# Masked cross attention: pairs of heads on halves of 64 rows, mask addition and maximum in one instruction, the output in a projection bank

## The reference

```python
h = _rmsnorm(hidden_states, ln1_w)
kv = _rmsnorm(kv_states, ln1_w)
q = (h @ Wq).reshape(bsz, q_len, NH, HD).transpose(0, 2, 1, 3)      # 16 heads of 64
k = (kv @ Wk).reshape(bsz, k_len, NKV, HD).transpose(0, 2, 1, 3)    # 4 heads of 64
v = (kv @ Wv).reshape(bsz, k_len, NKV, HD).transpose(0, 2, 1, 3)
q = _apply_rope(q, cos_q, sin_q)
k = _apply_rope(k, cos_k, sin_k)
k, v = repeat of each of the 4 heads for 4 query heads
scores = jnp.einsum('bhqd,bhkd->bhqk', q, k) / math.sqrt(HD)
scores = scores + attention_mask                                    # (8, 1, 112, 375)
probs = jax.nn.softmax(scores.astype(jnp.float32), axis=-1)
attn = jnp.einsum('bhqk,bhkd->bhqd', probs, v)
hidden = residual + attn.transpose(0, 2, 1, 3).reshape(bsz, q_len, NH * HD) @ Wo
```

## Time and profile before

| | us |
|---|---|
| three runs: median (lowest to highest) | 2206.13 (2204.8 to 2211.46) |
| the profiled execution | 2202.19 |
| its span | 2200.4 |
| TensorE matmul busy in the span | 1836.1 (83%) |
| VectorE | 1396.9 (63%) |
| ScalarE | 877.2 (40%) |
| GpSimd | 640.2 (29%) |
| mean granted clock of TensorE | 0.915 |

### The profile page before, as it was taken

One profiled execution on the slowest core, in us unless ns is written; L12 is line 12 of the kernel. 1 busy time (PEld: TensorE's weight loads), 2 busy tenths in 40 slices (PEclk: granted clock), 3 DMA queues, 4 the chain that ended last, 5 costly groups with the idle time before them and its releaser, 6 DMA issues.

```text
span 2200.4 us, 34499 instructions
## 1 busy us (share of the span) xinstructions
PE 1836.1 (83%) x10658; PEld 1321.1 (60%) x10658; DVE 1396.9 (63%) x3343; ACT 877.2 (40%) x2513; POOL 640.2 (29%) x710
## 2 busy tenths in 40 slices
PE   5969997399848779998879998877887779988978
PEld 4747775388736567776745554663445655655557
DVE  5856666111168756666756676676777876777765
ACT  4635553122236425554334443333332354444421
POOL 2235553200033335555300000220002243544433
PEclk9979998599969889999879999888998899999979
DMA  4100000388720000010100200110001000001000
GB/s 162 31 19 15 14 0 1 128 272 301 261 101 1 0 8 16 15 45 5 57 15 15 71 0 1 48 58 1 0 0 68 1 11 11 10 10 37 41 1 17
DMA packets 34247, 102.76 MB, mean 47 GB/s; under 512 B 2624, under 2 KB 25696, under 8 KB 26976
## 3 DMA queue, kind: packets, MB, share of 16 engines
q1 hardware_dynamic: 32608, 97.79, 12.9%
q0 software_dynamic: 1536, 3.67, 0.6%
HBM read 93.20 MB, written 8.26 MB: 46 GB/s over the span
## 4 chain that ended last, share of the span: by engine, by line
PE 60%; DVE 18%; issue 10%; ACT 4%; POOL 4%; DMA 3%; DVEq 0%; SPq 0%; POOLq 0%; ACTq 0%
PE ps L750 9%; PE ps L867 7%; PE ps L710 5%; PE ps L715 5%; PE ps L902 4%; PE ps L813 4%; PE ps L763 4%; PE ps L795 4%; PE ps L745 3%; PE ps L997 2%; POOL arena L1734 2%; PE ps L981 2%; DMA arena<-rows_hbm 2%; PE ps L790 2%; PE ps L702 2%
## 5 line engine op out<-in xcount | busy, mean ns | idle before, releaser
L1734 POOL TENSOR_TENSOR arena<-arena,rinv 112x375 f32<-112x375 f32 (+1 forms) x448 | 371.3, 829 | 563.6 <-DVE rinv L1411 555.6
L750 PE MATMUL ps<-arena 128*112 128x375 f32 (+1 forms) x1280 | 387.7, 411 | 20.0 <-ACT arena L1104 13.0
L763 PEld LDWEIGHTS ps<-cst,arena 112*125 112x125 f32 (+1 forms) x1408 | 216.2, 183 | 157.0 <-POOL arena L1734 55.0
L1104 ACT ACTIVATE arena<-ps,negmax 112x375 f32<-112x375 f32 (+1 forms) x384 | 190.2, 500 | 190.9 <-DVE negmax L1406 189.9
L1406 DVE TENSOR_REDUCE negmax<-ps 112x1 f32<-112x375 f32 (+1 forms) x288 | 159.4, 553 | 161.4 <-PE ps L750 161.1
L763 PE MATMUL ps<-cst,arena 112*125 112x112 f32 (+1 forms) x1408 | 229.2, 275 | 38.2 <-POOL arena L1734 37.9
L750 PEld LDWEIGHTS ps<-arena 128*112 128x112 f32 x1280 | 177.3, 183 | 65.7 <-issue 24.6
L1782 POOL TENSOR_TENSOR w_split_sb<-wml,w_split_sb 128x512 fp32r<-128x512 f32 (+1 forms) x40 | 44.8, 1121 | 575.2 <-ACT w_split_sb L1153 573.3
L1104 ACT ACTIVATE arena<-arena,negmax 112x112 f32<-112x112 f32 (+1 forms) x256 | 125.8, 493 | 171.3 <-DVE negmax L1406 171.2
L1420 DVE COPY arena<-ps 125x336 f32<-125x336 f32 x384 | 187.7, 489 | 2.3 <-PE ps L763 1.7
L867 PE MATMUL ps<-h_split_sb,w_split_sb 128*128 128x448 f32 x768 | 178.0, 381 | 8.3 <-DVE h_split_sb L1531 4.3
(11 more groups left out here) (198 smaller groups left out, 3035.8 us busy)
## 6 DMA issues: line engine op xcount, KB each, us to landing
wml<-in_wm_L_moe SPq DMA_DIRECT2D x21, 1028.0 KB, 5.6
wml<-in_wm_L_moe SPq DMA_DIRECT2D x21, 1024.0 KB, 6.1
craw<-in_ctx SPq DMA_DIRECT2D x40, 375.0 KB
wml<-in_wm_L_m SPq DMA_DIRECT2D x3, 3072.0 KB, 12.9
wat<-in_wa_L_ca SPq DMA_DIRECT2D x2, 2560.0 KB, 9.2
wml<-in_wm_L_m SPq DMA_DIRECT2D x2, 2048.0 KB, 9.6
rows_hbm<-wml SPq DMA_DIRECT2D x2, 1344.0 KB, 14.4
arena<-rows_hbm SPq DMA_DIRECT2D x21, 128.0 KB, 5.6
```

Of the source, the lines that this page charges most:

```text
L750: last = mm(ps[0:S, S_BANK + s % blk.s_banks, i * blk.nk:(i + 1) * blk.nk], qz[:, parity(b), head_of(u) if blk.dh == 16 else u], kT[:, par ...
L763: last = nc.tensor.transpose(ps[0:blk.kp, T_BANK + s % blk.t_banks, o:o + S], buf[:, i * blk.nk + q * blk.kp:i * blk.nk + (q + 1) * blk.kp ...
L1104: last = go(probs[0:S, s % blk.nprobs, i * nk:(i + 1) * nk], src[:, i * nk:(i + 1) * nk], ACT.Exp, bias=negmax[:, u:u + 1], accum_out=rows ...
L1734: pool.tensor_tensor(p3, p3, r3, ALU.mult).then_inc(scaled, 1)
```

## The change

All of it is for `L3_ca` alone; the other blocks keep their instructions.

- **Pairs.** In even steps TensorE issues the scores of units `s` and `s + 1`, in odd steps none. Each matmul has 64 rows: the first the upper half (rows 0 to 63), the second the lower (64 to 127), in different banks. `qz` holds two heads per block and no zeros, so one copy by ScalarE fills it per QT instead of two. `place` says which head a unit now is: the units of a pair belong to two key heads.
- **Three score banks.** `bank_at` cycles through banks 0, 1, 2, with 0 and 2 for units 14 and 15. The pair waits until the maximum of unit `s - 2` is done.
- **One instruction** (`tensor_tensor_reduce`) adds the mask, negates, writes `ms`, and accumulates the minimum, which is the negated maximum. The exponential takes `ms` with scale -1. What said `masked` now says `maxed`.
- **Reciprocals.** That of unit `s - 2` stands ahead of the maximum of unit `s`, behind its wait for scores. By it VectorE also knows that the exponential has read `ms[s % 2]`.
- **Output.** `project` runs in step 5 instead of 6, into bank 7, which the pieces XT, QP1, CT1, KP1, V1, QT1 and KT1 use too. CT0 moves from step 5 to 4.

```diff
 "L3_ca": dict(
-    plan={1: ["XT"], 2: ["QP0"], 3: ["QP1"], 5: ["CT0"], 6: ["CT1"], 7: ["KP0"], 8: ["KP1"], 9: ["V0"],
+    plan={1: ["XT"], 2: ["QP0"], 3: ["QP1"], 4: ["CT0"], 6: ["CT1"], 7: ["KP0"], 8: ["KP1"], 9: ["V0"],
           10: ["V1"], 11: ["QT0"], 12: ["QT1"], 13: ["KT0"], 14: ["KT1"]},
...
-    out_step=6, lag=3, s_banks=2, t_banks=2, w_banks=[7, 3], out_bank=2),
+    out_step=5, lag=3, s_banks=3, t_banks=2, w_banks=[7, 3], out_bank=7),
...
+PAIRS = ("L3_ca",)
...
+    def bank_at(self, s):
+        return (s % 3 if s < 14 else 2 * s - 28) if self.s_banks == 3 else s % self.s_banks
...
+        def place(blk, u):
+            if not blk.pairs or blk.keys_first:
+                return u
+            if blk.dh == 64:
+                return 8 * (u // 8) + 4 * (u % 2) + u % 8 // 2
...
-                            sp.wait_ge(masked, st["masked"] + (m - 1) * blk.units)
+                            sp.wait_ge(maxed, st["turn"] + (m - 1) * blk.units)
...
                 def scores(b, s):
-                    free = masked if blk.mask else exped
-                    base = st["masked"] if blk.mask else st["unit"]
-                    wait(pe, free, count(base, units, b, s - blk.s_banks + 1))
+                    n = 2 if blk.pairs else 1
+                    free = masked if blk.mask == "causal" else maxed if blk.mask else exped
+                    base = st["masked"] if blk.mask == "causal" else st["turn"] if blk.mask else st["unit"]
+                    wait(pe, free, count(base, units, b, s + n - blk.s_banks))
...
+                    if blk.pairs:
+                        for z in range(2):
+                            bank = blk.bank_at(s + z)
...
+                                u = place(blk, s + z)
+                                rows = slice(64 * z, 64 * z + 64)
+                                mm(ps[0:S, bank, 0:blk.nk], qz[rows, parity(b), 4 * (u // 8) + u % 4],
+                                   kT[rows, parity(b), u // 8, 0:blk.nk], start=True, stop=True).then_inc(scored, 1)
+                        return
...
-                        if b != B:
+                        if b != B and (s % 2 == 0 or not blk.pairs):
                             scores(b, s)
...
                     elif name in ("QT0", "QT1"):
                         i = int(name[2])
-                        for z in range(2):
+                        if blk.pairs:
+                            last = go(qz[:, par, 4 * i:4 * i + 4], W[:, 0:4 * S].rearrange("p (r s) -> p r s", s=S), ACT.Identity, scale=0.125)
+                        for z in range(0 if blk.pairs else 2):
                             last = go(qz[:, par, 8 * i + 4 * z:8 * i + 4 * z + 4], W[:, 0:4 * S].rearrange("p (r s) -> p r s", s=S),
                                       ACT.Identity, scale=cs("mask64", 2)[:, z:z + 1])
...
-                                  bias=negmax[:, u:u + 1], accum_out=rowsum[:, u:u + 1])
+                                  scale=-1.0 if blk.mask == "input" else 1.0, bias=negmax[:, u:u + 1], accum_out=rowsum[:, u:u + 1])
...
                 def maxima(b, s):
                     par, half = parity(b), pair(b)
                     dve.wait_ge(scored, count(st["unit"], units, b, s + 1))
...
+                    if blk.mask == "input":
+                        if s == 0:
+                            dve.wait_ge(mask_loaded[par], half * 16 + 16)
+                        at = lagged(b, s, 2, units)
+                        if at:
+                            reciprocals(*at)
+                        v.tensor_tensor_reduce(ms[0:S, s % 2, 0:nk], ps[0:S, blk.bank_at(s), 0:nk], mask_sb[:, par], -1.0, 3.4028234e38,
+                                               ALU.add, ALU.min, negmax[:, s:s + 1]).then_inc(maxed, 1)
+                        return
                     if blk.mask:
                         wait(dve, exped, count(st["unit"], units, b, s - 1))
-                        if blk.mask == "input":
-                            if s == 0:
-                                dve.wait_ge(mask_loaded[par], half * 16 + 16)
-                            add = mask_sb[:, par].unsqueeze(1)
-                        else:
-                            add = cs("causal", S, S).unsqueeze(1).broadcast_to([S, HG, S])
+                        add = cs("causal", S, S).unsqueeze(1).broadcast_to([S, HG, S])
...
-                        last = v.tensor_copy(pT[0:kp, g % 4, :, s % HG], T_[:, 0:KC * S].rearrange("p (k s) -> p k s", s=S))
+                        last = v.tensor_copy(pT[0:kp, place(blk, s) // gu % 4, :, place(blk, s) % HG], T_[:, 0:KC * S].rearrange("p (k s) -> p k s", s=S))
...
                         at = lagged(b, s, 1, units)
-                        if at and not blk.keys_first:
-                            reciprocals(*at)
+                        if blk.mask == "input" and b == B and s < 2:
+                            reciprocals(*lagged(b, s, 2, units))
+                        elif at and not blk.keys_first:
+                            if blk.mask != "input":
+                                reciprocals(*at)
```

33 lines of the change are left out of this document (25 added, 8 removed).

## The result

The changed kernel takes 2164.16 us (median of four runs, 2161.83 to 2170.68) against 2205.79 (2204.80 to 2211.46) on the same chip: a ratio of 0.983, 95% interval 0.9804 to 0.9857. The forecast was 2176 with a range of 2156 to 2205. The time lies inside it and the sign is right, but 41.6 us were saved where 29.6 were forecast, so something was mis-sized.

A forecast was written before the change was run, and what follows sets the result against it. TensorE's work (34.6 us) plus waits, with VectorE nearly as loaded, bound a batch. Work 30.7, waits 6.6 and clock 2.6 gave 39.9 instead of 43.7; over eight batches 29.6 us saved, forecast 2176, range 2156 to 2205.

The forecast's parts named there:

- Scores in pairs, 0.78 us: TensorE's scores: two half-row matmuls run side by side, 0.78 us a pair instead of 1.26, 3.9 us off a batch.
- the walk: Step-by-step count of TensorE's waits through one batch: 6.6 us, practically the 6.5 of before.
- The new instruction, 0.55 us, step 1.02: VectorE: mask addition and maximum in one instruction of 0.55 us, so a step takes 1.02 us instead of 1.51.
- The rival at half rate: VectorE's new instruction takes two passes, steps of 1.46 us instead of 1.02: 2205 us in all; chance 0.10.
- serial pairs: TensorE's paired score matmuls run one after the other, 1.42 us a pair: 2202 us in all; chance 0.12.
- The reciprocal's place, not before 2.03 us: VectorE's reciprocal stands behind the wait for scores, so the odd step's turn starts at least 2.03 us after the pair.
- plus 2.6 for the clock: TensorE's half-speed stretches go on costing 2.6 us a batch, making 37.3 us into 39.9.
- my signs of being right: Paired scores start together; VectorE step about 1.02 us; weighs 39 to 41 us apart; clock 0.92 to 0.96.
- The rival of a falling clock: TensorE, less busy, sits at 1.2 GHz from step 12 to step 3: 2226 us, slower than before; chance 0.10.
- The last batch, 3.4 us saved: End of the stage: a loop of 2.1 us for two steps replaces VectorE's 1.51 a step, saving 3.4 us.
- Output in bank 7, third bank, ScalarE, mask: Remaining parts of the change: the moved output's waits are hidden, and the other three bring nothing of their own.
- more comes: In the eight batches the clock's cost halves and waits shrink by a fifth, 21 us more: 2156; chance 0.08.

The follow-up runs named there:

- e1: Kernel before with only the one instruction for mask and maximum, and the reciprocal of unit s - 2 ahead of it: 2161.2 us, ratio 0.980.
- e3: Changed kernel with each score matmul over all 128 rows again, same order, three banks, two QT copies: 2169.8 us, ratio 0.985.
- e2: Changed kernel with mask addition and maximum as two instructions again: 2193.1 us, ratio 0.996.
- e6: Changed kernel with the reciprocal of unit s - 2 ahead of VectorE's wait for scores, a one-column memset taking that wait: 2157.9 us, ratio 0.978.
- e7: Changed kernel with the statistics of all eight batches computed once behind the last update: 2156.2 us, ratio 0.978.

## Why the prediction was right or wrong

**What bounds the kernel.** Right. TensorE's work and waits set the batch and VectorE's work didn't, once the step was short: e1 has TensorE busy 97% of the batch.

**Scores in pairs, 0.78 us.** Right in mechanism: 0.82. I counted 3.9 us a batch off TensorE's work and put the waits that replace it into the walk, but never priced this part by itself. e3 says 0.4. So of the 3.9 us of work taken off nearly all came back as waits.

**The new instruction, 0.55 us, step 1.02.** Right: 0.53 + 0.08 with 0.45 from its start to the next, and a step of 0.95 to 1.0. The rival at half rate is out, and so is that of serial pairs. The rule of the Trainium skill quoted in the prediction ("DVE: opcode table, instruction layouts, handler registers and perf-mode slots", Datapath and trigger behaviour), that a stage reading its own last result has no bubble, agrees with the 0.45.

**The reciprocal's place, not before 2.03 us.** Right to the hundredth in most pairs of the rows above, 2.18 in one. The walk gave 30.7 + 6.6 = 37.3 at full clock, and 37.75 was measured at a clock of 1.00. The profile labels only 188.75 - 174.72 = 14.0 us, 2.8 a batch, as TensorE's idle time, since a turn's modelled 0.58 outlasts its 0.31 to 0.42 from start to start; the sum was checked, its split hardly. Where it can be checked, it is off: turn 13 and KT0 wait 0.5 us together and not 1.6, and the pairs with the turns behind them cost some 1.0 us a batch more than I counted (8 times 0.04 and 0.08). That these two cancel is luck.

**"plus 2.6 for the clock".** This is the step that failed. I carried the cost of the half-speed stretches over as a constant of the stage, because the waits stay as long in sum. They do not hang on the sum: e2 waits longer in sum than the kernel before and has a full clock. In the kernel before they stand behind the wait ahead of KT0 (2.07 us) in four of the five batches, and at QP0 in four of the five. In the five batches of the changed kernel the first of these waits is 0.27, QP0 no longer waits, and no stretch is slow. The walk itself had shortened the wait at KT0 (I wrote 1.6 for turn 13 and KT0 together; 0.25 and 0.27 came), and still I left the clock as it was. What exactly sets it is open, as e6 shows. Of my signs of being right two failed with this term: the weighs lie 37.75 us apart and not 39 to 41, and the clock is 1.00 and not 0.92 to 0.96. The rival of a falling clock had the sign wrong for the same reason: it went by the busy share, and e2 has a smaller share than before at full clock. With the clock at full, 5 x 2.6 = 13 us more than forecast were to be had; 10.7 came.

**The last batch, 3.4 us saved.** Wrong sign, -2.7. Two terms were mis-sized. The loop of two steps was put at 2.1 us and takes 2.54 (2064.35 to 2066.89) at full clock: 2.03 and then the odd turn, 0.51, which the next pair stands behind. By the walk's own formula that is 0.24 a step and 2.2 for nine, not 0.4 and 3.6. And the chain of statistics, with the clock behind it, was named nowhere: I counted what was moved (the projection and the update) and not what hangs behind it on its engine. In the changed kernel it costs 3.96 us of wait and then a clock of 0.77 over 35.7 us, where the kernel before had 2.89 and 0.87 over 33.0. By (1 - clock) times the time, my estimate, that is 8.2 against 4.3 us, so 3.9 of the 6.1 that are missing. e7 shows the price of the chain there, 8.3 us. That it comes from the earlier step is not shown, since e1 and e3 have the chain in either place and end in 31.2 and 31.7 us.

**Output in bank 7, third bank, ScalarE, mask.** No wait of the projection, of CT1 or for `out_done` shows in the five batches: hidden, as said. The third bank was not tried alone; with the new order and the moved output it made a batch with full rows 0.7 us longer (e1 to e3), where I gave it nothing.

**The rival "more comes"** (a chance of 0.08) is what happened in the middle of the stage, in its first term alone: the clock's cost went to nothing and not to a half, and the waits stayed. The first batch and the five gave 13.5 us more than forecast; the last gave 6.1 less.
